# Quantised self-attention: who sums the fourth head's exponentials

## The reference, cut to what matters

```python
B, H, DH = 8, 16, 8           # batches, heads, width of a head; 256 queries, 256 keys
h = _ln(x, ln1_g, ln1_b)
q, k, v = (h @ wq, h @ wk, h @ wv)                 # split into 16 heads
sim = einsum('bhid,bhjd->bhij', fq(q, dq, 128), fq(k, dk, 128)) * DH ** -0.5
attn = softmax(sim, axis=-1)                       # exp(sim - max) / sum
out = einsum('bhij,bhjd->bhid', fq(attn, dw, 0), fq(v, dv, 128))
x = x + out @ wo + bo
# fq(t, d, z): round(t / d) + z, clipped to 0..255, minus z, times d
```

## Time and profile before

| | us |
|---|---|
| runs | 1162.77, 1159.96, 1157.63 |
| median | 1159.96 |
| profiled execution, own time | 1158.71 |
| its span | 1156.9 |
| PE busy | 947.6 |
| DVE busy | 807.9 |
| ACT busy | 623.2 |
| POOL busy | 498.3 |

### The profile page before, as it was taken

How to read it: one execution, slowest core, us unless ns; L and a number is a source line. 1 busy time by engine, 2 the same in 40 slices (tenths; PEclk the granted TensorE clock), 3 DMA queues, 4 the chain that set the end, 5 groups by cost and what they waited for, 6 DMA issues and landing times.

```text
span 1156.9 us, 24615 instructions
## 1 busy us (share of the span) xinstructions
PE 947.6 (82%) x8666; PEld 583.4 (50%) x8666; DVE 807.9 (70%) x1832; ACT 623.2 (54%) x1509; POOL 498.3 (43%) x966
## 2 busy tenths in 40 slices
PE   2798898855557989898986899999888779887996
PEld 1344444433334545465553566666545446565664
DVE  4788888787757556544475776767546667888887
ACT  1777777688841245423352445455335457666674
POOL 2677777856533243132131753226544331334312
PEclk9999755555569989988697999999969979999998
DMA  8300000000000000000000000000000000000000
GB/s 274 117 1 1 0 0 2 1 1 1 1 1 1 0 1 2 1 1 1 1 2 1 2 2 2 1 0 1 2 1 2 1 1 1 1 11 0 9 2 19
DMA packets 13505, 13.57 MB, mean 12 GB/s; under 512 B 4696, under 2 KB 10208, under 8 KB 13280
## 3 DMA queue, kind: packets, MB, share of 16 engines
q1 hardware_dynamic: 13408, 12.29, 3.5%
HBM read 11.24 MB, written 1.05 MB: 11 GB/s over the span
## 4 chain that ended last, share of the span: by engine, by line
PE 48%; DVE 26%; ACT 9%; issue 9%; POOL 6%; DMA 1%; DVEq 1%; SPq 0%; ACTq 0%; POOLq 0%
ACT sb_E L1132 5%; PE ps_context L698 4%; POOL sb_E L2127 3%; PE ps_scores L755 3%; PE ps_scores L777 3%; PE ps_context L701 3%; DVE sb_E L1857 2%; DVE sb_neg_raw L1418 2%; PE ps_rounds L885 2%; DVE sb_inv_den L1658 2%; PE ps_turned L971 2%; PE ps_turned L608 2%; PE ps_scores L588 2%; PE ps_turned L1030 1%; PE ps_scores L960 1%
## 5 line engine op out<-in xcount | busy, mean ns | idle before, releaser
L1132 ACT ACTIVATE sb_E<-ps_scores,sb_neg_max,sb_score_scale 128x256 f32<-128x256 f32 (+1 forms) x384 | 190.9, 515 | 64.3 <-DVE sb_neg_max L1421 63.9
L2127 POOL TENSOR_SCALAR sb_E<-sb_E,sb_inv_sum 128x256 f16<-128x256 f32 x256 | 124.1, 485 | 47.2 <-DVE sb_inv_sum L1460 29.5
L1362 ACT ACTIVATE sb_E<-ps_scores,sb_ff_bias 128x512 f32<-128x512 f32 x128 | 87.6, 688 | 67.6 <-PE ps_scores L1018 65.2
L1626 DVE TENSOR_REDUCE sb_neg_half<-ps_scores 128x16 f32<-128x1024 f32 x48 | 58.7, 1222 | 80.3 <-PE ps_scores L755 80.3
L1857 DVE TENSOR_TENSOR sb_E<-sb_E 128x512 f16<-128x512 f32 x128 | 93.1, 745 | 28.0 <-ACT sb_E L1365 25.8
L1030 PE MATMUL ps_turned<-sb_moe_down,sb_E 128*128 128x128 f16 x512 | 93.5, 221 | 23.0 <-DVE sb_E L1857 22.8
L1418 DVE TENSOR_REDUCE sb_neg_raw<-ps_scores 128x4 f32<-128x1024 f32 (+1 forms) x80 | 97.3, 1216 | 14.1 <-PE ps_scores L588 12.0
L1160 ACT ACTIVATE sb_E<-ps_scores 128x512 f32<-128x512 f32 x96 | 57.3, 598 | 86.2 <-PE ps_scores L692 85.6
L1031 PE MATMUL ps_turned<-sb_moe_down,sb_E 128*128 128x128 f16 x512 | 93.1, 220 | 0.0
L1032 PE MATMUL ps_turned<-sb_moe_down,sb_E 128*128 128x128 f16 x512 | 93.1, 220 | 0.0
L1443 DVE TENSOR_REDUCE sb_neg_quad<-ps_scores 128x2 f32<-128x512 f32 (+1 forms) x96 | 64.5, 683 | 34.2 <-PE ps_scores L649 34.1
(11 more groups left out here) (286 smaller groups left out, 2480.5 us busy)
## 6 DMA issues: line engine op xcount, KB each, us to landing
sb_moe_up<-in_moe_up SPq DMA_DIRECT2D x1, 2048.0 KB
sb_rows<-in_rows SPq DMA_DIRECT2D x1, 1216.0 KB, 7.8
out_x<-sb_raw_context SPq DMA_DIRECT2D x8, 128.0 KB, 1.8
sb_X<-in_x SPq DMA_DIRECT2D x1, 768.0 KB, 9.9
sb_square<-in_square SPq DMA_DIRECT2D x1, 768.0 KB, 11.1
sb_ctxT<-in_ctxT SPq DMA_DIRECT2D x1, 512.0 KB, 11.2
sb_stacked<-in_stacked SPq DMA_DIRECT2D x1, 512.0 KB, 7.2
sb_ff_up<-in_ff_up SPq DMA_DIRECT2D x1, 512.0 KB, 4.6
```

The costliest lines, as they stand in the source:

```text
L1132: last = act.activation(E[:, ring, head], SC[t % 2][:, head], ACT.Exp, bias=neg_max[:, ring, h:h + 1], scale=scale, accum_out=row_sum[:, r ...
L1362: last = act.activation(U_full[:, k % 4, :], banks[k % 4], ACT.Gelu, bias=bias, scale=1 / WEIGHT_SCALE)
L2127: last = pool.tensor_scalar(E16[:, ring, SEQ * h:SEQ * h + SEQ], E[:, ring, SEQ * h:SEQ * h + SEQ], inv_sum[:, ring, h:h + 1], HALF, ALU.m ...
```

## The change

Of a unit's four heads the fourth (index 3 = SUMMED) is no longer summed by ACT: its ACTIVATE has no `accum_out`. `invert_sums` on DVE sums that head's 256 exponentials for both units of a pair with one reduction (128 x 2 x 256 elements of E in SBUF, to 128 x 2 of row_sum), raises `row_summed`, waits for it, and goes on with the scaling as before. For a2 the same lines do what they did. `row_summed` is now counted in a1 as well.

```diff
+SUMMED = 3
@@ counts
         c["raw_max"] = n
+        c["row_summed"] = n // 2
         if not layer.over_self:
-            c.update(subbed=n, row_summed=n // 2, rounded=n, q_cast=NBATCH, v_cast=NBATCH)
+            c.update(subbed=n, rounded=n, q_cast=NBATCH, v_cast=NBATCH)
@@ quant_exps (ACT)
                 for h in range(L.heads if L.over_self else BIASED):
                     head = slice(L.keys * h, L.keys * h + L.keys)
-                    last = act.activation(E[:, ring, head], SC[t % 2][:, head], ACT.Exp,
-                                          bias=neg_max[:, ring, h:h + 1], scale=scale,
-                                          accum_out=row_sum[:, ring, h:h + 1])
+                    if L.over_self and h >= SUMMED:
+                        last = act.activation(E[:, ring, head], SC[t % 2][:, head], ACT.Exp,
+                                              bias=neg_max[:, ring, h:h + 1], scale=scale)
+                    else:
+                        last = act.activation(E[:, ring, head], SC[t % 2][:, head], ACT.Exp,
+                                              bias=neg_max[:, ring, h:h + 1], scale=scale,
+                                              accum_out=row_sum[:, ring, h:h + 1])
@@ invert_sums (DVE)
                 dve.wait_ge(S["exped"], B["exped"] + n + 2)
                 sums = row_sum[:, ring, 0:L.heads]
-                if not L.over_self:
-                    dve.tensor_reduce(row_sum[:, ring, BIASED:], E[:, ring, CTX * BIASED:].rearrange(
-                        "p r (h k) -> p r h k", k=CTX), AX.X, ALU.add).then_inc(S["row_summed"], 1)
-                    dve.wait_ge(S["row_summed"], B["row_summed"] + pair + 1)
+                first = SUMMED if L.over_self else BIASED
+                dve.tensor_reduce(row_sum[:, ring, first:L.heads], E[:, ring, L.keys * first:].rearrange(
+                    "p r (h k) -> p r h k", k=L.keys), AX.X, ALU.add).then_inc(S["row_summed"], 1)
+                dve.wait_ge(S["row_summed"], B["row_summed"] + pair + 1)
```

## The result

The changed kernel takes 1169.64 us (median of 4, 1168.79 to 1177.48) against 1159.53 before (median of 4): ratio 1.0099, 95% interval 1.005 to 1.0148. It is 10.1 us slower. Single runs of one kernel lie up to 12 us apart here, so for the steps I read one length in each trace: layer a1 from DVE's first maximum to its hT for the next layer. It is 224.22 - 24.02 = 200.20 us before and 235.16 - 24.41 = 210.75 after, +10.55. Another 0.39 us lie ahead of a1, so it ends 10.94 us later, and the span grew by 10.0. So the loss lies in a1; the layers behind were shifted and are 0.9 us shorter in all.

What follows compares the result with a forecast made beforehand. DVE was taken to pace layer a1 most of the time. First batch 1.05, six batches 9.84 and last 2.6 gave 13.5 us, added to 1159.96: 1173.5, rounded to 1173, range 1163 to 1182.

Steps and rivals of the forecast that it cites:

- The accumulator read at 0.09, not 0.20: ACT's last exponential of each unit: release 0.09 us earlier without the read, though its row shows 0.20.
- Step 0 free: Insertion at step 0 of a repeated batch: its 0.72 us hides in the landing's wait of 1.00 to 1.07.
- Step 5's wait gone, that of 1.20 unchanged: Step 5's landing loses its 0.43 us wait for transposes; step 0's maximum keeps its 1.20 us round trip over hT.
- A batch of 27.0 us: Each of a1's six repeated batches grows from 25.34 us by 1.64.
- the first 1.05: First batch, three insertions: one covered, one 0.33, one whole at 0.72; 1.05 us in all.
- the last 2.6: From 199.7 on, five insertions, 3.60 us, less a wait of 0.56 and 0.09 each; 2.6 us.
- the terms of 0.63, 0.29 and 0.72 for steps 2, 4 and 6: Net delays in us per repeated batch from the insertions at these steps, after covers; together 1.64.
- The recorded sum with a free wait: The skill page's case: semaphore wait costs nothing, an insertion 0.58 us, the whole 10.0 us, some 1170.
- PE's 88%: PE's busy share in the six repeated batches, distrusted because 8 transposes are shown longer when they have waited.
- POOL's lag costs nothing: POOL's normalising starts later, but has four steps' lag and idles 22.3 us, so it was costed at nothing.
- DVE paces: DVE paces layer a1 most of the time, 86% busy in the repeated batches; ACT mostly waits.
- ACT paces: Rival: exponential, scores, maximum is last at every unit, each earlier release counts, 5.8 us faster, 1154; chance 0.06.

Runs made afterwards that it cites:

- e1: ACT's part alone against before: fourth head has no accumulator and nobody sums it, a constant stands in; 1147.1 us, ratio 0.9907.
- e9: Before with all its instructions, but the fourth head's sum goes to a spare column and a constant 100.0 is used; 1150.85 us, ratio 0.9937.
- e2: DVE's part alone against before: ACT keeps all four accumulators, DVE adds the reduction for each pair; 1173.83 us, ratio 1.0153.
- e3: Before with the change only for pairs whose sum falls into step 0 of a batch; 1159.08 us, ratio 1.0021.
- four parts: Four runs against before, each with the change for pairs of one step only (0, 2, 4, 6); ratios 1.0021, 1.0056, 1.0028, 1.0042.
- e6: Changed kernel with the landing put between the reduction and its wait in steps 2, 4 and 6; 1165.34 us, ratio to before 1.0065.
- e5: Changed kernel with the reduction done twice in a row for every pair; 1189.18 us, ratio to before 1.0241.
- e8: Changed kernel with the scaling of the sums moved from DVE to POOL; 1164.99 us, ratio to before 1.006.
- e10: Changed kernel with both scaling on POOL and the landing between reduction and wait; 1163.74 us, ratio to before 1.0038.
- e7: Before with the scaling of the sums moved from DVE to POOL; 1160.07 us, ratio 1.0015.

## Why the prediction was right

It said 1173, 1163 to 1182, slower; it is 1169.64. Its mechanism held in the places it named, and its sum was 3 us too high, more than a quarter of the effect.

- *The price of an insertion*, 0.68 and 0.04 behind it: measured 0.681 and 0.04.
- *The accumulator read at 0.09, not 0.20*: 0.54 against 0.45 from start to start. All 64 of them brought 1.1 us (e1 against e9) or 0.83 (the changed kernel against e2), 0.05 to 0.07 in a quiet batch: the earlier release counts at about one place in eight.
- *Step 0 free*: -0.01 in the mean, 0.04 in a quiet batch (e3), the wait down to 0.35 as foretold. *Step 5's wait gone, that of 1.20 unchanged*: so it is.
- *A batch of 27.0 us*: 27.13. But I had 25.34 + 1.64, and it is 25.65 + 1.48. The mean of 25.34 hid that the sixth batch is shorter: with nothing left to prepare it has no round trip over hT. It takes 23.80 and grew by 0.92.
- *The mis-sized terms* are those of the sum, 13.5 us against 10.55: six batches 9.84, measured 8.35 (five of 1.48, one of 0.92); the first 1.05, measured 0.64; the last 2.6, measured 1.56. The rows of DVE place the differences. In a quiet batch of the changed kernel the terms of 0.63, 0.29 and 0.72 for steps 2, 4 and 6 are 0.49, 0.23 and 0.71, and 0.12 more come between step 0 and step 2: 1.55 for 1.64. One tenth at step 2 is the scaling behind ACT's release, 0.33 us before and 0.23 in the changed kernel (111.99). In the first batch the three insertions cost -0.18, 0.35 and 0.47 for 0, 0.33 and 0.72. In the last, the one of step 6 cost 0.10 for 0.63, and the three ahead of it 0.84 for 1.33; the one behind it was paid as foretold. The third of the first batch and that one share a cause that the sum didn't have: in before DVE's L1421 ahead of them took 0.48 and 0.59 us beside an addition on POOL, and in the changed kernel, which comes later there, 0.23 (last section). The 0.17 us by which a quiet batch exceeds its four parts stays open.
- *The wait's price.* The recorded sum with a free wait, 10.0, comes nearer to 10.55 than 13.5 does. That is chance: e6 got 3.5 us back from the waits, and what was too high are the terms above.
- *PE's 88%* was set aside with a reason that the rows don't bear out: 8 transposes take 1.03 to 1.06 us nearly everywhere, and 0.62 at 128.63, behind a wait too. That DVE sets the pace of a1 rests on e2, e5 and e6 instead.
- *POOL's lag costs nothing*: true of the change as far as the landings show, which wait 2.2 us, though PE's waits for POOL rose from 10.0 to 12.5, which was named as a sign of being wrong. With 0.28 us more work a pair on POOL and a wait behind it, the landings' waits are 5.1 us (e8) and 6.8 (e10).
- *DVE paces* was half of the truth. Going up it was right, and e5 shows it for a second reduction. Going down (e7) it was wrong: by the rows at step 3, exponential, scores and maximum form a chain as long as DVE's own work. I had weighed "ACT paces" at 0.06 as something for every unit; in fact it holds at some units already and forbids a gain there.

## What to carry to other kernels

Before moving work between engines, see who waits for whom: here ACT waited 41 us for DVE, and the change gave DVE more. Price an accumulator read by the distance from start to start (0.09 us), not by its row (0.20). An added instruction costs its duration less the first wait behind it whose releaser doesn't hang on it, so look for that wait and put the instruction there; and an engine that looks like the bound may be level with a chain, so that adding costs in full and removing brings little. Where a wait on the instruction right before must stay, put an independent instruction between the two: 0.13 us a place here.

## What the runs showed of the hardware that I had not expected

- Other values in the tiles went with another time. With the instructions of before, one write more at the start and another sum for one head of four in the first layer, the kernel took 1150.85 us against 1157.51 (ratio 0.9937, 0.9903 to 0.9971). In the profiled executions most of it lies behind a1, and 3.1 us in two stretches where the granted clock was 1.00 and 0.84 (e9) against 0.73 and 0.72 (before), so it comes in part by the course of PE's clock. The mean over the span hides this (0.844 in e9, 0.859 in before). What in the data sets that course stays open. A kernel that leaves out part of the computation needs a control with the same data.
- The granted clock of the trace isn't PE's speed in a1. Two batches of the kernel before, at 1.00 (2.4 GHz) and at 0.50 (1.2 GHz), hold the same 158 matmuls and last 25.62 us both, with the same busy time of PE:

```profile
97.23:122.85 25.62, 22.97 (x158) 12.03 (x158) 21.95 (x47) 18.52 (x66) 19.06 (x40) 1.00 0.00 1
148.64:174.26 25.62, 22.96 (x158) 12.02 (x158) 21.96 (x46) 18.52 (x66) 19.06 (x40) 0.50 0.00 0
```

A pair of scores takes 1.03 us in both, and 0.60 in a short stretch between them:

```profile
127.67 1.03 PE L588 MATMUL ps_scores<-sb_KBD,sb_QS 32*128 32x512 f16 x2
...
129.41 0.60 PE L588 MATMUL ps_scores<-sb_KBD,sb_QS 32*128 32x512 f16 x2
```

So the two batches don't show that a1 could do with a slower PE; they show that PE was as fast in one as in the other.

- A small DVE instruction takes longer beside an addition on POOL. In before, the 4 of 64 scaled maxima (L1421) that run beside POOL's L2101 take 0.48 to 0.59 us. Of the 60 others 42 take 0.23 to 0.25, and the longest 0.47. One of before with its neighbour on POOL, then its like in the changed kernel, clear of it:

```profile
217.30 0.59 DVE L1421 TENSOR_SCALAR sb_neg_max<-sb_neg_raw,sb_neg_scale 128x4 f32<-128x4 f32 x1
217.15 0.72 POOL L2101 TENSOR_TENSOR sb_X<-sb_X,sb_rows 128x256 f32<-128x256 f32 x1
```

```profile
227.52 0.23 DVE L1427 TENSOR_SCALAR sb_neg_max<-sb_neg_raw,sb_neg_scale 128x4 f32<-128x4 f32 x1
227.79 0.73 POOL L2107 TENSOR_TENSOR sb_X<-sb_X,sb_rows 128x256 f32<-128x256 f32 x1
```
